# A two-layer gated cross-attention and mixture-of-experts kernel: the last router steps in another order, and identity products between them

## The chip, the core and the metric

The kernel runs on one core of a Trainium2 chip. The metric is the device time of one execution in microseconds (us). The core has five engines that run side by side, each with its own queue of instructions in program order: TensorE (PE, matrix products; its weight loads are shown as PEld), VectorE (DVE), ScalarE (ACT), GpSimd (POOL) and SyncE (SP, which issues most transfers). They wait for each other on semaphores. An instruction that waits holds up everything behind it on its own engine.

## The reference, cut to what matters

The input is `x`, eight sequences of 256 rows with 256 values each, and a context of the same number of rows with 192 values. Two layers follow. Each has a cross-attention with 16 heads and a feed-forward part with eight experts:

```python
x = x + tanh(g_xattn[0]) * L0_xattn(layernorm(x), ctx)
x = x + tanh(g_ffn[0])   * L0_ffn(layernorm(x))       # all 8 experts, 4 weighted, and a shared one
x = x + tanh(g_xattn[1]) * L1_xattn(layernorm(x), ctx)
x = x + tanh(g_ffn[1])   * L1_ffn(layernorm(x))       # 2 of 8 experts for each row
```

The last line is the one that matters here. The router computes eight logits for each row (`layernorm(x) @ Wr + br`), takes the two largest, and weighs them by a softmax. Each row then goes through its two experts, `relu(x @ W1[e] + b1[e]) @ W2[e] + b2[e]`.

## The kernel before

The attention of both layers is cut into 16 units, one for each layer and sequence (`UNITS`), and each unit into eight pairs of heads. For a pair, PE computes the scores by query, DVE takes their row maximum, PE computes the scores by key, ACT takes the exponentials, DVE clips them in the second layer, and PE weighs the values (`weigh_values`, two pairs at a time). Then come `take` (ACT copies the sums), `turn_values` (PE transposes them, DVE divides), `attn_turn` (PE), `project` (PE, then DVE). For the last unit, number 15, the product of `project` is added to `x` on DVE (L1353).

The order of the work is a table, `PLAN`. `make_plan` puts each stage at a half-slot number, and every engine walks through the numbers and issues its own part of each stage. Nothing else decides the order. A slot holds one pair's scores by query, one pair's scores by key, and the stages of two numbers. The scores by key of unit 15 stand in slots 148 to 155.

The second layer's feed-forward part is prepared sequence by sequence. `pick_z` and `stats` finish the row sums and their moments (DVE and POOL), `normal` (ACT) writes the normalized rows, `turn` (PE, copied by ACT) transposes them, `logits1` (PE) multiplies them with the router's weights, and DVE ranks the eight logits and writes `mask` and `picks`. `count1` (PE) adds up on one bank, `by_query[:, 0, :]`, how many rows before each row chose each expert. `weights1` is the softmax, `bias_turn` and `bias1` add the experts' second bias to `x`. `sums` prepares two sums of the last sequence ahead of its projection.

Once all eight sequences are counted, `blocks` and `tables` (DVE) work out which expert each of the 23 blocks of 256 places belongs to, and where each row stands. `stand_at` writes matrices `at_place` that are one where a row stands at a place; `early_places` does that ahead of time for the sequences that are counted by then, `tables` for the rest. A product (L916) turns them into token numbers, POOL gathers the rows, and then the blocks run: `turn_rows`, `up`, `down` (PE), with three products for each matrix product since both sides are split into a high and a low part.

Three banks of PSUM are shared in turn by the small stages (`share_banks`). A stage that takes a bank waits for the stage that had it before.

## Time and profile before

| what | value |
|---|---|
| median of 3 runs | 1027.02 us (1021.71 to 1029.29) |
| the profiled execution | 1020.56 us |
| its span, first to last instruction | 1018.7 us |
| mean granted TensorE clock in it | 0.903 of full |
| PE, DVE, ACT, POOL busy | 89%, 73%, 48%, 24% of the span |

The profile comes from one execution. A row of the timeline gives the start in us from the span's start, the duration in us, the engine, the line of the kernel, the operation, what it writes and reads, and how many instructions are taken together; behind it may stand how long the engine was idle before and what ended the wait. The granted clock is the share of TensorE's full clock of 2.4 GHz: 0.5 is 1.2 GHz. An ordinary float32 product stands in the trace as two instructions, so that x8 means four products.

### The profile page before, as it was taken

What the parts mean: (1) busy time and instruction counts of PE and PEld (TensorE: products, weight loads), DVE (VectorE), ACT (ScalarE), POOL (GpSimd) and SP (SyncE); (2) the same over time, 40 slices, a digit from 0 to 9 for tenths busy, and PEclk for the clock granted to TensorE, in tenths of its full rate; (3) what the DMA queues carried; (4) which work ended last, traced back from release to release, by engine and by line L of the source; (5) the groups of instructions that cost most, each with busy time, mean ns of one, the idle gap of its engine ahead of it and who ended that gap; (6) DMA issues with size and microseconds to landing.
All of it is one profiled execution on the core that took longest, in us unless ns stands there. A gap on an engine that the chain in (4) does not pass through costs nothing.

```text
span 1018.7 us, 18031 instructions
## 1 busy us (share of the span) xinstructions
PE 903.4 (89%) x6385; PEld 735.6 (72%) x6385; DVE 748.5 (73%) x1494; ACT 486.2 (48%) x842; POOL 241.9 (24%) x390
## 2 busy tenths in 40 slices
PE   3578999999999998999888888975699999999995
PEld 2355777777776776677665555643699999999995
DVE  3445667777676768988878789757598888888872
ACT  2135544444534443434434444431376666776762
POOL 5011111020210000101010133320524444444433
PEclk9569899999999999999999766665599999999998
DMA  6967786056154263738374873421666677776642
GB/s 154 167 131 134 173 198 133 25 99 106 43 71 76 45 118 75 140 103 134 85 148 94 220 154 98 122 75 34 235 222 208 212 232 228 231 227 220 208 146 31
DMA packets 129866, 141.52 MB, mean 139 GB/s; under 512 B 12561, under 2 KB 122281, under 8 KB 129649
## 3 DMA queue, kind: packets, MB, share of 16 engines
q1 hardware_dynamic: 119296, 127.59, 51.2%
q0 software_dynamic: 8832, 12.25, 5.6%
q8 instruction: 51, 0.84, 0.4%
q10 hardware_dynamic: 1648, 0.53, 0.2%
q14 instruction: 39, 0.31, 0.1%
HBM read 109.45 MB, written 30.36 MB: 137 GB/s over the span
## 4 chain that ended last, share of the span: by engine, by line
PE 66%; DVE 21%; issue 5%; ACT 3%; POOL 2%; DMA 1%; POOLq 0%; DVEq 0%; ACTq 0%
PE bank L966 12%; PE bank L802 8%; PE by_query L950 7%; PE by_key L950 7%; DVE rowmax L1298 5%; PE bank L812 4%; PE value_bank L744 4%; PE bank L650 4%; PE by_query L707 3%; DVE probs L1323 3%; PE bank L693 3%; PE bank L771 2%; PE bank L659 2%; PE by_key L726 2%; DVE stats L1253 1%
## 5 line engine op out<-in xcount | busy, mean ns | idle before, releaser
L1102 ACT ACTIVATE probs<-by_key 128x1024 f32<-128x1024 f32 x128 | 130.7, 1021 | 92.2 <-PE by_key L726 91.4
L1298 DVE TENSOR_REDUCE rowmax<-by_query 128x4 f32<-128x1024 f32 x128 | 155.4, 1214 | 17.0 <-PE by_query L707 16.9
L1791 POOL TENSOR_SCALAR rstd<-moments 128x2 f32<-128x2 f32 x32 | 10.5, 328 | 514.9 <-DVE moments L1257 514.9
L1851 POOL DMA_INDIRECT out_x<-x,token_i x46 | 78.0, 1695 | 146.8 <-ACT x L1208 139.8
L966 PE MATMUL bank<-w_hi,h_hi 128*128 128x256 f32 x368 | 104.1, 283 | 0.0
L966 PE MATMUL bank<-w_lo,h_hi 128*128 128x256 f32 x368 | 104.1, 283 | 0.0
L966 PE MATMUL bank<-w_hi,h_lo 128*128 128x256 f32 x368 | 104.1, 283 | 0.0
L707 PE MATMUL by_query<-stack_k,stack_q 48*128 48x256 f32 x512 | 70.9, 358 | 35.6 <-DVE rowmax L1298 35.3
L707 PEld LDWEIGHTS by_query<-stack_k,stack_q 48*128 48x128 f32 x512 | 42.8, 206 | 76.7 <-DVE rowmax L1298 46.9
L744 PE MATMUL value_bank<-probs,values 128*32 128x256 f32 x1024 | 79.4, 433 | 8.9 <-DVE probs L1323 8.8
L812 PE MATMUL bank<-w_down,hidden 128*128 128x256 f32 x288 | 79.9, 401 | 3.7 <-DVE summed L1361 1.8
L1323 DVE SCALAR_TENSOR_TENSOR probs<-probs,lower 128x1024 f32<-128x1024 f32 x64 | 77.9, 1218 | 7.1 <-DMA lower<-lower 7.1
L802 PE MATMUL bank<-xnT,w_gate 128*128 128x256 f32 x288 | 78.8, 397 | 3.0 <-DVE lo L1289 2.4
L1135 ACT ACTIVATE act_gate<-bank 128x256 f32<-128x256 f32 x72 | 27.6, 383 | 103.6 <-PE bank L802 103.6
L802 PE MATMUL bank<-xnT,w_up 128*128 128x256 f32 x288 | 74.2, 380 | 0.0
L1456 DVE SCALAR_TENSOR_TENSOR x<-bank,expert_cols,x 128x256 f32<-128x256 f32 x144 | 62.4, 474 | 15.2 <-PE bank L812 15.2
L966 PEld LDWEIGHTS bank<-w_hi,h_hi 128*128 128x128 f32 x368 | 70.7, 192 | 0.0
L966 PEld LDWEIGHTS bank<-w_lo,h_hi 128*128 128x128 f32 x368 | 70.7, 192 | 0.0
L966 PEld LDWEIGHTS bank<-w_hi,h_lo 128*128 128x128 f32 x368 | 70.7, 192 | 0.0
L1720 DVE TENSOR_TENSOR h_lo<-x,h_hi 128x512 fp32r<-128x512 f32 x92 | 63.7, 693 | 3.2
L802 PEld LDWEIGHTS bank<-xnT,w_gate 128*128 128x128 f32 x288 | 52.9, 194 | 15.6 <-DVE lo L1289 3.4
L1690 DVE TENSOR_TENSOR w_lo<-w,w_hi 128x2048 fp32r<-128x2048 f32 x23 | 52.7, 2292 | 15.4 <-ACT w_hi L1173 15.4
(242 smaller groups left out, 2147.7 us busy)
## 6 DMA issues: line engine op xcount, KB each, us to landing
w<-in_L_ffn_W SPq DMA_DIRECT2D x46, 1024.0 KB, 8.7
lower<-lower SPq DMA_DIRECT2D x64, 256.0 KB, 5.3
stack_k<-qk SPq DMA_DIRECT2D x96, 128.0 KB, 5.2
stack_q<-qk SPq DMA_DIRECT2D x96, 128.0 KB, 7.0
qk<-hi SPq DMA_DIRECT2D x31, 256.0 KB, 2.9
qk<-lo SPq DMA_DIRECT2D x31, 256.0 KB, 2.6
rows<-w_gate SPq DMA_DIRECT2D x8, 264.0 KB, 4.6
x<-in_x SPq DMA_DIRECT2D x8, 256.0 KB, 7.0
```

Of the source, the lines that this page charges most:

```text
L707: mm = pe.matmul(by_query[:, side, t * S:t * S + S], sq[rows, p, t * P:t * P + P], sk[rows, p, :], start=True, stop=True)
L744: mm = pe.matmul(value_bank[32 * c:32 * c + 32, o:o + S], values[u % 2][:, kt, 4 * j + c, :], probs[(i + c // 2) % 4][:, kt, c % 2, :], st ...
L802: mm = pe.matmul(bank[:, half * S:half * S + S], w[:, k, e, :], turned_of(("ffn0", b))[:, k, :], start=k == 0, stop=k == 1)
L812: mm = pe.matmul(bank[:, t * D:t * D + D], hidden0[i % 6][:, t * P:t * P + P], w_down0[:, e, :], start=True, stop=True)
L950: mm = pe.matmul(up_bank[pair][:, half * SLOTS:half * SLOTS + SLOTS], wt[:, k, j * P:j * P + P], xt[:, k, :], start=n == 0, stop=n == len( ...
L966: mm = pe.matmul(bank[:, t * D:t * D + D], ht[:, j, t * P:t * P + P], wt[:, j, :], start=j == 0 and t == 0 and n == 0, stop=j == JH - 1 an ...
L1102: ac.activation(probs[i % 4][:, :, :, :].rearrange("p k h s -> p h k s"), by_key[:, :, :].rearrange("p h (k s) -> p h k s", k=2), ACT.Exp) ...
L1298: dv.tensor_reduce(rowmax[u % 2][:, :, p, :], by_query[:, :, :].rearrange("p h (t s) -> p h t s", t=TT), AX, ALU.max).then_inc(sem.max_don ...
L1323: dv.scalar_tensor_tensor(prob, prob, 1.0, bound, ALU.min, ALU.max).then_inc(sem.clip_done, 1)
L1456: op = dv.scalar_tensor_tensor(xt, bank[:, t * D:t * D + D], expert_cols[b % 2][:, t, e:e + 1], xt, ALU.mult, ALU.add)
L1720: dv.tensor_tensor(hl[:, part, :], relu[pair], hh[:, part, :].bitcast(F32), ALU.subtract).then_inc(sem.h_lo, 1)
L1851: po.indirect_dma_start(out[:, :], bass.IndirectOffsetOnAxis(ap=token_i[:, n:n + 1].bitcast(U32), axis=0), ysb[i % 3][:, t, :], None, comp ...
```

## The change

`make_plan` moves the router steps of the last but one sequence, number 6, behind the last unit's values. `EARLY` goes from 14 to 12 row tiles of 128 rows: `early_places` covers six sequences and no longer seven. It is cut in two: part 0 works out the places and writes `at_place` for the first pick, part 1, later, for the second. `bias_turn` and `bias1` of sequence 6 come late, beside those of sequence 7. `sums` comes after the router of sequence 6.

PE gets a new function, `stay_busy`. It issues n products of the identity matrix with itself, 128 rows by 128 columns in float32, into the half `by_query[:, 1, :]` that nobody reads any more. 102 of them are put in: 49 by the table `IDLE_PRODUCTS`, each group ahead of PE's part of the stage that it names, 18 in six groups of three at the ends of slots 150 to 155, and 35 in three groups around the tokens and the first rows. Two banks change places (`turn_bank`, `down_bank`), since the token product now takes another one of the three.

```diff
--- before.py
+++ after.py
@@ -36,7 +36,7 @@
 BLOCKS = NB * S * TOPK1 // SLOTS + E1 - 1
 COLS = BLOCKS * BT
 PICKS = TOPK1 * NT
-EARLY = NT - TT
+EARLY = NT - 2 * TT
 WIDE = D + E1
 CLAMP = 10000.0
 EPS = 1e-5
@@ -63,6 +63,17 @@
 
 FIRST = [("stats", ("query", 0)), ("ctx", 0), ("normal", ("query", 0)), ("gates", 0), ("scale_queries", 0), ("turn", ("query", 0)),
          ("kprod", 0), ("stack_keys", 0), ("qprod", 0), ("stack_queries", 0)]
+
+
+
+IDLE_PRODUCTS = {("turn", ("finish", NB - 2)): 3,
+                 ("logits1", NB - 2): 1,
+                 ("attn_turn", UNITS - 1): 2,
+                 ("project", UNITS - 1): 3,
+                 ("turn", ("finish", NB - 1)): 13,
+                 ("logits1", NB - 1): 2,
+                 ("count1", NB - 1): 9,
+                 ("bias_turn", NB - 1): 16}
 
 
 def layer_of(u):
@@ -141,19 +152,21 @@
         at[g].append(("pick_z", b))
         at[g + 2].append(("stats", ("finish", b)))
         at[g + (9 if b == NB - 1 else 4)].append(("normal", ("finish", b)))
-        at[g + 6 ].append(("turn", ("finish", b)))
-        at[g + 8 ].append(("logits1", b))
-        at[g + 9 ].append(("soft1", b))
-        at[max(g + 10 , 2 * base(UNITS) + 1 + b)].append(("count1", b))
+        behind = 4 if b == NB - 2 else 0
+        at[g + 6 + behind].append(("turn", ("finish", b)))
+        at[g + 8 + behind].append(("logits1", b))
+        at[g + 9 + behind].append(("soft1", b))
+        at[max(g + 10 + 3 * behind // 2, 2 * base(UNITS) + 1 + b)].append(("count1", b))
         if b == NB - 1:
-            at[g - 8].append(("sums", b))
-            at[g - 2].append(("early_places", 0))
+            at[g - 7].append(("early_places", 0))
+            at[g - 2].append(("sums", b))
+            at[g + 5].append(("early_places", 1))
             at[g + 11].append(("blocks", 0))
             at[g + 12].append(("tables", 0))
-        at[g + 11 ].append(("weights1", b))
-        late = 5 if b == NB - 2 else 0
-        at[g + 13 + late].append(("bias_turn", b))
-        at[g + 15 + late].append(("bias1", b))
+        last_but_one = b == NB - 2
+        at[g + (21 if last_but_one else 11)].append(("weights1", b))
+        at[g + (25 if last_but_one else 13)].append(("bias_turn", b))
+        at[g + (31 if last_but_one else 15)].append(("bias1", b))
     return at
 
 
@@ -239,7 +252,7 @@
     value_bank = es.enter_context(nc.psum_tensor("value_bank", [P, 512], F32))
     banks = [es.enter_context(nc.psum_tensor(f"bank{i}", [P, 512], F32)) for i in range(3)]
     up_bank = [by_query[:, 0, :], by_query[:, 1, :], by_key[:, 0, :], by_key[:, 1, :]]
-    turn_bank, down_bank = [value_bank, banks[0]], [banks[1], banks[2]]
+    turn_bank, down_bank = [value_bank, banks[1]], [banks[0], banks[2]]
 
     x = sb("x", [P, NT, D])
     ident = sb("ident", [P, P])
@@ -623,6 +636,11 @@
                 pe.wait_ge(by_name[freed[0]], freed[1])
             return banks[no]
 
+        def stay_busy(n, bank):
+
+            for _ in range(n):
+                pe.matmul(bank[:, 0:P], ident[:, :], ident[:, :], start=True, stop=True)
+
         def ctx(u):
             if layer_of(u):
                 return
@@ -854,7 +872,7 @@
             counts = by_query[:, 0, :]
             if b == 0:
                 pe.wait_ge(sem.max_done, PAIRS * UNITS)
-            if b == NB - 1:
+            if TT * b == EARLY:
                 pe.wait_ge(sem.table_chain, 1)
             pe.wait_ge(sem.mask_ready, b + 1)
             for t in range(TT * b, TT * b + TT):
@@ -900,14 +918,22 @@
                 scores_by_key(u, p)
             for stage, n in PLAN[2 * g]:
                 if stage in stages:
+                    if (stage, n) in IDLE_PRODUCTS:
+                        stay_busy(IDLE_PRODUCTS[stage, n], by_query[:, 1, :])
                     stages[stage](n)
             u, p = divmod(g - base(0) - LAG - 3, PAIRS)
             if 0 <= u < UNITS and p % 2 == 0:
                 weigh_values(u, p // 2)
             for stage, n in PLAN[2 * g + 1]:
                 if stage in stages:
+                    if (stage, n) in IDLE_PRODUCTS:
+                        stay_busy(IDLE_PRODUCTS[stage, n], by_query[:, 1, :])
                     stages[stage](n)
-
+            if base(UNITS - 1) + LAG + 1 < g < base(UNITS) + LAG:
+                pe.wait_ge(sem.max_done, PAIRS * UNITS)
+                stay_busy(3, by_query[:, 1, :])
+
+        stay_busy(10, by_query[:, 1, :])
         pe.wait_ge(sem.tile_no, 2)
         pe.wait_ge(sem.at_place_ready, TOPK1)
         for i, (tile, r) in enumerate((tile, r) for tile in range(NT) for r in range(TOPK1)):
@@ -968,7 +994,9 @@
                                        skip_group_check=True)
             mm.then_inc(sem.down_mm, 1)
 
+        stay_busy(20, by_query[:, 1, :])
         turn_rows(0)
+        stay_busy(5, by_query[:, 1, :])
         up(0, range(0, 2))
         turn_rows(1)
         up(0, range(2, 4))
@@ -1564,16 +1592,19 @@
         def tabled():
             dv.wait_ge(sem.table_chain, chain[0])
 
-        def stand_at(places, first_tile, end):
+        def stand_at(places, first_tile, end, which=range(TOPK1)):
             shape = [P, end - first_tile, P]
-            for r in range(TOPK1):
+            for r in which:
                 dv.tensor_tensor(at_place[:, r, first_tile:end, :], places[:, r, :].unsqueeze(2).broadcast_to(shape),
                                  place_row[:, :].unsqueeze(1).broadcast_to(shape), ALU.is_equal).then_inc(
                     sem.at_place_ready, 1)
 
-        def early_places(_):
-
-            dv.wait_ge(sem.counted, NB - 1)
+        def early_places(part):
+
+            if part:
+                stand_at(early_place[:, :, :], 0, EARLY, range(part, TOPK1))
+                return
+            dv.wait_ge(sem.counted, EARLY // TT)
             dv.wait_ge(sem.qk2_done, PAIRS * UNITS)
             table(dv.tensor_tensor(slots_pick[:, :, 0:EARLY, :], picks[:, :, 0:EARLY, :],
                                    by_query[:, 0, 0:EARLY * E1].rearrange("p (t e) -> p t e", e=E1).unsqueeze(1)
@@ -1588,7 +1619,7 @@
             tabled()
             table(dv.tensor_copy(early_place[:, :, :].rearrange("p r t -> p (r t)"), slot_i[:, 1, 0:TOPK1 * EARLY]))
             tabled()
-            stand_at(early_place[:, :, :], 0, EARLY)
+            stand_at(early_place[:, :, :], 0, EARLY, range(1))
 
         def blocks(_):
             dv.wait_ge(sem.counted, NB)
```

How PE's queue looks from the scores of unit 15's last pair but one on. Before (`bank<-wr,xnT` are the logits of `logits1`, `bank<-ident,w_gate 128x128` is the turn of the normalized rows of sequence 6, `bank<-ident,weighted` the turn of the values, `bank<-ident,attn` is `attn_turn`, and `bank<-wo,attnT` the projection):

```order
L726 MATMUL by_key<-stack_q,stack_k 128x256 x4
L744 MATMUL value_bank<-probs,values 32x256 x8
L684 MATMUL bank<-ident,w_gate 128x128 x4
L849 MATMUL bank<-wr,xnT 128x8 x4
L744 MATMUL value_bank<-probs,values 32x256 x8
L861 MATMUL by_query<-mask,tri 128x8
...
L754 MATMUL bank<-ident,weighted 128x128 x4
L763 MATMUL bank<-ident,attn 128x128 x4
L771 MATMUL bank<-wo,attnT 128x256 x4
```

Now, with the identity products as `by_query<-ident`:

```order
L744 MATMUL by_key<-stack_q,stack_k 128x256 x4
L762 MATMUL value_bank<-probs,values 32x256 x8
L642 MATMUL by_query<-ident 128x128 x3
L762 MATMUL value_bank<-probs,values 32x256 x8
L642 MATMUL by_query<-ident 128x128 x3
L702 MATMUL bank<-ident,w_gate 128x128 x4
L772 MATMUL bank<-ident,weighted 128x128 x4
L642 MATMUL by_query<-ident 128x128
L867 MATMUL bank<-wr,xnT 128x8 x4
L642 MATMUL by_query<-ident 128x128 x2
L781 MATMUL bank<-ident,attn 128x128 x4
L642 MATMUL by_query<-ident 128x128 x3
L789 MATMUL bank<-wo,attnT 128x256 x4
```

The last values went ahead of the turn and the logits of sequence 6, the turn of the values ahead of the logits, and the count of sequence 6 (`mask,tri`) behind the projection.

PE's queue from the turn of the last sequence (`bank<-ident,w_up`) to the tokens. Before:

```order
L684 MATMUL bank<-ident,w_up 128x128 x4
L849 MATMUL bank<-wr,xnT 128x8 x4
L861 MATMUL by_query<-mask,tri 128x8
...
L876 MATMUL bank<-ident,w_gate 8x128 x2
L884 MATMUL bank<-b,wT 128x256 x2
L916 MATMUL bank<-in_tile_no,at_place 128x92 x32
```

Now:

```order
L642 MATMUL by_query<-ident 128x128 x13
L702 MATMUL bank<-ident,w_up 128x128 x4
L642 MATMUL by_query<-ident 128x128 x2
L867 MATMUL bank<-wr,xnT 128x8 x4
L894 MATMUL bank<-ident,w_gate 8x128 x2
L642 MATMUL by_query<-ident 128x128 x9
L879 MATMUL by_query<-mask,tri 128x8
...
L642 MATMUL by_query<-ident 128x128 x16
L894 MATMUL bank<-ident,w_gate 8x128 x2
L902 MATMUL bank<-b,wT 128x256 x4
L642 MATMUL by_query<-ident 128x128 x10
L942 MATMUL bank<-in_tile_no,at_place 128x92 x32
```

Fifty identity products came in here (13, 2, 9, 16 and 10), and two sequences' bias products (x4) stand ahead of the tokens instead of one's.

DVE's queue behind unit 15's last clip, up to the row sums of the last sequence. Before, the router and the early places (both picks) ran there, the places behind the divided values (`attn<-bank,recip`) and right ahead of the projection's sum (L1353):

```order
L1323 SCALAR_TENSOR_TENSOR probs<-probs,lower 128x1024 x2
L1528 TENSOR_TENSOR route_0<-bank,br 128x16
...
L1335 TENSOR_TENSOR attn<-bank,recip 128x2x128
...
L1570 TENSOR_TENSOR at_place<-early_place,place_row 128x1792 x2
L1353 SCALAR_TENSOR_TENSOR x<-bank,tg,x 128x512
```

Now:

```order
L1351 SCALAR_TENSOR_TENSOR probs<-probs,lower 128x1024 x2
L1609 TENSOR_TENSOR slots_pick<-picks,by_query 128x2x96
...
L1598 TENSOR_TENSOR at_place<-early_place,place_row 128x1536
...
L1363 TENSOR_TENSOR attn<-bank,recip 128x2x128
L1556 TENSOR_TENSOR route_0<-bank,br 128x16
...
L1381 SCALAR_TENSOR_TENSOR x<-bank,tg,x 128x512
...
L1598 TENSOR_TENSOR at_place<-early_place,place_row 128x1536
L1553 SCALAR_TENSOR_TENSOR route_1<-bank,rstd,br 128x8 x2
```

One of the two early place matrices now stands ahead of the divided values and the other behind the projection's sum.

## Rows read from the trace of the kernel before

**Rows 1.** The page: busy time by engine, and granted clock in 40 slices

```profile
PE 903.4 (89%) x6385; PEld 735.6 (72%) x6385; DVE 748.5 (73%) x1494; ACT 486.2 (48%) x842; POOL 241.9 (24%) x390
PEclk9569899999999999999999766665599999999998
```

**Rows 2.** Windows, PE: stretch, length, busy (instructions), granted clock, DMA share, GB/s

```profile
646.80:670.50 23.70, 23.20 (x141) 0.50 0.53 130
670.70:677.40 6.70, 5.28 (x43) 1.00 0.39 110
677.50:697.90 20.40, 13.41 (x68) 0.50 0.11 32
701.40:735.40 34.00, 18.59 (x102) 0.50 0.47 158
```

**Rows 3.** Timeline, unit 15's last clips to its projection, all engines

```profile
678.60 2.35 DVE L1323 SCALAR_TENSOR_TENSOR probs<-probs,lower 128x1024 f32<-128x1024 f32 x2
681.94 1.09 ACT L1062 ACTIVATE w_gate<-x,rstd 128x256 f32<-128x256 f32 x2 [4.24 <-POOL rstd L1798]
683.17 1.08 PE L684 MATMUL bank<-ident,w_gate 128*128 128x128 f32 x4 [3.10 <-ACT w_gate L1062]
685.10 1.85 PE L849 MATMUL bank<-wr,xnT 128*128 128x8 f32 x8 [0.84 <-ACT xnT L1079]
686.87 1.94 PE L744 MATMUL value_bank<-probs,values 128*32 128x256 f32 x16
688.94 0.60 ACT L1109 ACTIVATE weighted<-value_bank 128x512 f32<-128x512 f32 x1 [3.99 <-PE value_bank L744]
689.68 1.09 PE L754 MATMUL bank<-ident,weighted 128*128 128x128 f32 x4 [0.29 <-ACT weighted L1109]
...
693.66 3.75 PE L771 MATMUL bank<-wo,attnT 128*128 128x256 f32 x8 [0.84 <-ACT attnT L1116]
693.74 3.96 DVE L1570 TENSOR_TENSOR at_place<-early_place,place_row 128x1792 bf16<-128x1792 f32 x2
697.62 0.74 DVE L1353 SCALAR_TENSOR_TENSOR x<-bank,tg,x 128x512 f32<-128x512 f32 x1
```

**Rows 4.** Timeline, PE at the full clock, shortly before

```profile
672.33 1.07 PE L744 MATMUL value_bank<-probs,values 128*32 128x256 f32 x16
674.82 0.66 PE L754 MATMUL bank<-ident,weighted 128*128 128x128 f32 x4
```

**Rows 5.** Timeline, from the last sequence's turn to its count

```profile
701.13 0.92 PE L684 MATMUL bank<-ident,w_up 128*128 128x128 f32 x4 [1.59 <-DVE w_up L1262]
702.89 1.85 PE L849 MATMUL bank<-wr,xnT 128*128 128x8 f32 x8 [0.84 <-ACT xnT L1079]
704.95 0.36 DVE L1525 SCALAR_TENSOR_TENSOR route<-bank,rstd,br 128x8 f32<-128x8 f32 x2 [3.36 <-PE bank L849]
707.20 0.17 PE L861 MATMUL by_query<-mask,tri 128*128 128x8 bf16 x1 [2.46 <-DVE mask L1537]
```

**Rows 6.** Timeline, from the last bias turn to the first rows

```profile
711.20 0.59 PE L876 MATMUL bank<-ident,w_gate 128*8 128x128 f32 x2 [3.73 <-DVE w_gate L1551]
712.40 2.04 PE L884 MATMUL bank<-b,wT 8*128 8x256 f32 x4 [0.61 <-ACT wT L1042]
716.28 0.75 DVE L1570 TENSOR_TENSOR at_place<-place_tile,place_row 128x256 bf16<-128x256 f32 x2
716.42 2.63 PE L916 MATMUL bank<-in_tile_no,at_place 128*128 128x92 bf16 x32 [1.98 <-DVE in_tile_no L1639]
717.22 0.68 DVE L1510 TENSOR_TENSOR x<-bank,x 128x512 f32<-128x512 f32 x1
718.99 3.60 PE L923 MATMUL bank<-onehotT,b 8*128 8x23 f32 x16
719.10 0.39 DVE L1679 TENSOR_SCALAR tok<-bank,spare_row 128x23 f32<-128x23 f32 x2 [1.20 <-PE bank L916]
726.97 1.12 PE L934 MATMUL value_bank<-ident,xs_in 128*128 128x128 f32 x4 [4.37 <-DMA xs_in<-rows,token_i]
```

**Rows 7.** Chain of waits: two equal groups of the first block's products

```profile
729.50 5.49 PE by_query L950 x24
...
735.72 2.87 PE by_key L950 x24
```

## The prediction

> **What bounds the kernel now.** I read the page first [rows 1]: PE is busy for 89% of the span, and its granted clock is full or nearly so except in the first slices and in a stretch from slice 24 to 29. The change acts in that stretch alone. The windows [rows 2] cut it up: the clock is 0.50 from 646.8 to 670.5 us although PE is busy for 23.20 of 23.70 us, 1.00 for the next 6.7 us, and 0.50 again from 677.5 to 697.9 and from 701.4 to 735.4 us. So a first stretch is bound by PE at half its clock, and two others are chains through several engines in which PE works and waits by turns, also at half clock.
>
> The timeline gives the chain [rows 3]. DVE ends the last clip at 680.95 (678.60 + 2.35). The last values could start then. But PE stands at the turn of sequence 6, which needs ACT's normalized rows (681.94 + 1.09), and the values wait behind turn and logits until 686.87. From the last clip to the projection's sum on DVE (697.62) it takes 16.67 us. Then the last sequence's sums, turn, logits and router follow [rows 5], the tables, the tokens, the gather and the first products [rows 6].
>
> **What an identity product costs.** No such product is in the trace before. The nearest row is the projection, also float32 on the full array: four products of 256 columns take 3.75 us at half clock [rows 3], 0.94 each. Half the columns make 0.47 us, and 0.23 at full clock. The lower bound is a transpose of 128 columns: 1.09 / 4 = 0.27 us at half clock [rows 3] and 0.66 / 4 = 0.17 at full clock [rows 4]. I take 0.47 and 0.23, since a transpose is another kind of instruction. 102 products are then 24 us of PE at full clock and 48 at half. Most of it lies in waits; what it does to the time depends on the clock that is granted, so I work out each term at both.
>
> **A, slots 150 and 151.** Two groups of three stand ahead of unit 14's projection, and PE is the bound there [rows 2]. At half clock they add 6 x 0.47 = 2.8 us. If they bring the clock up one step earlier, some 6 us of PE at half clock are halved, less the groups themselves at mixed clock: about -1.4. The other four groups stand where PE waits anyhow (5.28 busy of 6.70 us [rows 2]), in 1.4 us of gaps, and I count them at nothing if the clock is full. I take 0, between the ends.
>
> **B, from the last clip to the projection's sum.** Counted from the last clip's end, at full clock: values until 1.2 (1.07 us [rows 4]); three products; the turn of sequence 6, which needs ACT's rows at 2.1 (683.03 - 680.95), until 2.9; the turn of the values (0.66) until 3.5; DVE is then busy with the early places until about 3.2 (small steps of 1.5 us together, and one matrix of 1536 columns for 3.96 / 2 x 1536 / 1792 = 1.7 us), so nothing waits for it; one product, the logits (half of 1.85) until 4.7; two products; `attn_turn` until 5.8; ACT's copy (0.60 and 0.1 for the hand-over) until 6.5, with three products beside it; the projection (half of 3.75) until 8.4. The sum starts at 8.6 instead of 16.67: -8.1 us. The router of sequence 6 and the two sums need about 3.5 us of DVE from 4.8 on, and end before 8.6. At half clock the same walk gives 2.1, 3.5, 4.6, 5.7, 8.0 (one product and the logits), 10.1 (two products, `attn_turn`), 11.5 (three products outlast ACT) and 15.3: -1.4 us. A half-clock piece inside a mostly full stretch costs 1 to 2 us. I take -7.0, nearer the full clock, since the gaps that PE has now (7.0 of 20.4 us idle [rows 2]) are nearly all filled or closed.
>
> **C, the last turn and logits.** Now 7.33 us from the sum to the ranks [rows 5]. At full clock the turn saves 0.3 and the logits 0.9: -1.2. Thirteen products (3.0 us) fit behind the count of sequence 6 into the 3.5 us between 697.62 and 701.13. The second early matrix ends about 5.9 us after the sum and the logits reach DVE at 6.1, so it is hidden, barely; it is late next. At half clock thirteen products take 6.1 us and the turn starts 2.8 late. I take -0.6.
>
> **D, the count.** PE waits 2.46 us for the mask [rows 5]. Nine products and the bias turn of sequence 6 take 2.4 at full clock and 4.8 at half: 0 to +2.4. I take +0.4.
>
> **E, the tokens.** They start at 716.42, when DVE's `in_tile_no` is done [rows 6]. Ahead of them PE now has, from 707.4 on, sixteen products (3.7), the bias turn (which needs 711.2 anyhow), two bias products instead of one, ACT's copy between them, and ten products. At full clock that ends about 717, hidden but for 0.4 us, and then the tokens take 1.4 instead of 2.63. DVE meanwhile has two matrices of 512 columns (0.65 each instead of 0.37) and two additions of 0.68 [rows 6], and reaches `tok` at 719.25 instead of 719.10: +0.15. But the clock is 0.50 all through this stretch in the trace, the bias products in it included (2.04 us for two) [rows 2, 6], and the change puts more of them there. With the clock down there, the ten products take 4.7 us, the tokens start at 719 to 720 and take up to 2.6: +1.9 to +3.3. At half clock in all of it, with sixteen products of 7.5 us, the tokens start 8.6 us late. I take +1.9.
>
> **F, the first rows.** From the tokens' end (719.05) to the rows' arrival (726.97) there are 7.9 us that PE does not set [rows 6]. The bias products of the first layer of experts (3.60 at half clock, 1.8 at full) and twenty products (4.6 or 9.4) stand there: 6.4 us fit, 13.0 are 5.1 too many. Behind it the turn saves 0.5 at full clock and the first 24 products take 2.87 instead of 5.49 [rows 7]: -3.1 together. With the clock down at first and up later, the fill ends 2 to 3 us late and takes nearly all of that back. I take -1.7. From 735.5 on the clock is full in both and nothing changes.
>
> **Sum.** 0 - 7.0 - 0.6 + 0.4 + 1.9 - 1.7 = -7.0 us. The profiled execution took 1020.56 us, which makes 1013.6. It is 6.5 us below the median of the three runs shown, so against that median the forecast is 1027.0 - 7.0 = **1020 us**. SP's queue has the same transfers, two of them later and off the chain; POOL's is unchanged.
>
> **The rule on the clock, weighed.** In this trace the clock stood at 0.50 for 23.7 us of nearly unbroken PE work and rose only behind it [rows 2]. The Trainium skill (TensorE: Matmul & The Clock Gate, section "Why this matters for your kernels") says that an idle gap between bursts of products is what puts the clock down, and that back-to-back work keeps it up. The trace does not bear that out, since the busy stretch was at half clock too. By the rule the filled stretch would be at full clock throughout, which is the second case below.
>
> **Rivals.**
> 1. *Mixed clock*, the sum above: -3 to -11 us, 1016 to 1024. For it: every fill is sized for the full clock, but the rows at 0.50 include stretches in which PE had little idle time. Chance 0.50.
> 2. *Full clock nearly everywhere.* A -1.4, B -8.1, C -1.2, D 0, E +0.15, F -3.1: -13.6 us, 1013. This is what the rule named above would do. For it: a late fill at half clock makes its own stretch dense, and dense stretches are where the clock rose [rows 2, 7]. Against it: 646.8 to 670.5 was dense too. Chance 0.27.
> 3. *The fill gives back what the order gains.* The last values start 5.8 us earlier (686.87 to 681.05), but with the clock down in most of A and B, nine products stand on B's path. A +2.0, B -3.0, C 0, D +0.4, E +1.9, F 0: +1.3, that is 0 to +3 us, 1027 to 1030. For it: half clock is what three of four windows show [rows 2]. Chance 0.16.
> 4. *Slower.* Identity products do not raise the clock at all, like the transposes and values around 683 to 693 us [rows 2, 3], and every group longer than its wait delays what stands behind it on PE. A +2.8, B -1.4, C +2.8, D +2.4, E +8.6, F +5.1 and 0.9 for the five products behind the turn: +21 us, 1048. It decides as soon as thirteen products take over 3.1 us and sixteen with ten over what DVE's tables leave. Against it: those transposes stood between gaps, and the clock rose in the first block's unbroken products, 5.49 us for 24 of them and then 2.87 [rows 7]. Chance 0.07.
>
> **How the numbers follow.** The forecast is case 1's. Cases 1 and 2 and most of 3 must be in the range: 1010 to 1030 us, which leaves out case 4 and the tails. A difference under 1% (10.3 us) cannot be told from no change in this kernel. Faster by over 1% is below 1016.8: most of case 2 and a little of case 1, 0.29. Slower by over 1% is case 4, 0.07. The rest is 0.64.
>
> **What would show it.** In the new profile the last values should start within 0.3 us of the last clip, and the projection's sum 8 to 10 us behind that clip rather than 16.7 (B). An identity product should show as two instructions of together 0.23 or 0.47 us. Granted clock 1.00 between the last clip and the count says B and C are right; 0.50 in the bias products of sequences 6 and 7 and late tokens say E is; PE still in its twenty products when the rows land says that F is nearer 0. A clock of 0.50 throughout the fill would mean case 4. The forecast is wrong if the stretch ahead of unit 14's projection moves by more than the 2.8 us of A, or if the new places on DVE, not PE, set the ranks of the last sequence.

## The result

The changed kernel takes **1019.36 us** (median of 14 runs, 1009.17 to 1033.51) against 1026.41 us (14 runs, 1021.33 to 1030.36). The ratio is 0.9906, 95% interval [0.9877, 0.9936]. A second set (experiment 9) gave 1018.66 us (12 runs) against 1027.11 and 0.9879 [0.9844, 0.9914]. The medians count all runs; the ratios, here and below, leave out slow ones, those more than 1.5% above the fastest run of their kernel. The forecast against the median was 1020 us, a change of -7.0; measured were -7.1 and -8.5.

The profiled execution took 1020.99 us, no less than that of before (1020.56). Yet it holds the gain, and to see that one has to know where to measure. The page first, against [rows 1]:

```profile
PE 923.8 (91%) x6589; PEld 756.7 (74%) x6589; DVE 750.2 (74%) x1494; ACT 486.0 (48%) x842; POOL 241.4 (24%) x390
PEclk9667899999999999999999856769899999999998
```

PE is busy 20.4 us longer, in 204 more instructions. The granted clock is now low in slices 24 to 27 instead of 24 to 29. Then the windows of PE that answer to [rows 2] (stretch, length, busy time with instructions, granted clock, DMA share, GB/s):

```profile
675.00:682.30 7.30, 7.30 (x48) 0.67 0.51 151
682.30:691.40 9.10, 8.20 (x78) 1.00 0.33 82
691.40:700.00 8.60, 7.99 (x69) 1.00 0.00 1
700.00:709.60 9.60, 7.70 (x71) 1.00 0.09 30
...
716.20:719.90 3.70, 3.70 (x21) 0.65 0.84 290
...
723.50:729.90 6.40, 6.40 (x42) 0.73 0.21 60
```

From the sum of unit 14's projection on, the clock is full except in the ten products ahead of the tokens and the start of the tokens, and again in part of the twenty products; the experts' bias products between them run at full clock (1.96 us for 16 instructions, 3.60 before [rows 6]). I measure from unit 15's first scores by key to the first product of `down`. Before, this takes 93.11 us (651.51 to 744.62), now 84.71 (660.66 to 745.37): 8.4 us less. But the stretch began 9.15 us later, in a part that the change does not touch, where the clock stood lower in this execution (0.90 on average ahead of the stretch, 0.91 before). Behind `down` both need 274 us. The pieces, against the profile of before (a projection's sum is DVE's addition of it, the ranks are DVE's first step on the logits (`route`), the count is DVE's reading of it):

| piece | before | after | change | predicted |
|---|---|---|---|---|
| A, first scores to the sum of unit 14's projection | 20.39 | 21.69 | +1.3 | 0 |
| that sum to the last clip's end | 9.06 | 9.05 | 0 | 0 |
| B, last clip to the sum of unit 15's projection | 16.66 | 8.65 | -8.0 | -7.0 |
| C, sum to ranks | 7.33 | 7.10 | -0.2 | -0.6 |
| D, ranks to count | 2.57 | 2.48 | -0.1 | +0.4 |
| E, count to `tok` | 11.58 | 12.18 | +0.6 | +1.9 |
| `tok` to the first rows' turn | 7.87 | 9.02 | +1.15 | 0 |
| F, that turn to the second 24 products | 8.51 | 5.40 | -3.1 | -1.7 |

**B** in the timeline of the changed kernel, the rows that answer to [rows 3]:

```profile
689.04 2.35 DVE L1351 SCALAR_TENSOR_TENSOR probs<-probs,lower 128x1024 f32<-128x1024 f32 x2
691.45 1.07 PE L762 MATMUL value_bank<-probs,values 128*32 128x256 f32 x16 [0.93 <-DVE probs L1351]
692.41 1.09 ACT L1090 ACTIVATE w_gate<-x,rstd 128x256 f32<-128x256 f32 x2 [2.72 <-POOL rstd L1829]
692.45 0.94 PE L642 MATMUL by_query<-ident 128*128 128x128 f32 x6
693.64 0.63 PE L702 MATMUL bank<-ident,w_gate 128*128 128x128 f32 x4 [0.26 <-ACT w_gate L1090]
695.11 1.03 PE L867 MATMUL bank<-wr,xnT 128*128 128x8 f32 x8
697.96 1.96 PE L789 MATMUL bank<-wo,attnT 128*128 128x256 f32 x8 [0.17 <-ACT attnT L1144]
700.04 0.75 DVE L1381 SCALAR_TENSOR_TENSOR x<-bank,tg,x 128x512 f32<-128x512 f32 x1 [0.37 <-PE bank L789]
```

The last values start 0.06 us behind the last clip (691.39) instead of 5.9 us. The three identity products (x6, since each is two instructions) take 0.94 us while ACT's rows are still on their way. The turn, the logits and the projection take little over half of what they took [rows 3], and before the projection PE waits 0.17 us instead of 0.84. **C**, against [rows 5]:

```profile
699.92 3.15 PE L642 MATMUL by_query<-ident 128*128 128x128 f32 x26
704.11 1.75 DVE L1598 TENSOR_TENSOR at_place<-early_place,place_row 128x1536 bf16<-128x1536 f32 x1
704.40 1.52 POOL L1825 TENSOR_TENSOR rstd<-rstd 128x2 f32<-128x2 f32 x1
705.04 1.03 PE L867 MATMUL bank<-wr,xnT 128*128 128x8 f32 x8 [0.39 <-ACT xnT L1107]
707.15 0.36 DVE L1553 SCALAR_TENSOR_TENSOR route<-bank,rstd,br 128x8 f32<-128x8 f32 x2 [1.29 <-POOL rstd L1829]
```

The logits are there at 706.07, 6.0 us behind the sum as worked out. The ranks wait 1.1 us more, for POOL: its step of 128x2 at 704.40 takes 1.52 us, beside DVE's new matrix. The first **gather**, then, against [rows 6]:

```profile
719.91 1.86 PE L942 MATMUL bank<-in_tile_no,at_place 128*128 128x92 bf16 x32
721.80 0.39 DVE L1710 TENSOR_SCALAR tok<-bank,spare_row 128x23 f32<-128x23 f32 x2 [0.66 <-PE bank L942]
723.05 2.29 DVE L1721 TENSOR_TENSOR w_lo<-w,w_hi 128x2048 fp32r<-128x2048 f32 x1 [0.26 <-issue]
723.69 0.32 ACT L1242 ACTIVATE b_all<-bank 128x184 f32<-128x184 f32 x1 [1.07 <-PE bank L949]
723.74 2.71 POOL L1869 DMA_INDIRECT xs_in<-rows,token_i  x1 [16.73 <-DVE token_i L1717]
725.85 2.29 DVE L1721 TENSOR_TENSOR w_lo<-w,w_hi 128x2048 fp32r<-128x2048 f32 x1 [0.50 <-ACT w_hi L1201]
726.75 2.24 POOL L1869 DMA_INDIRECT xs_in<-rows,token_i  x1 [0.30 <-issue]
730.83 0.66 PE L960 MATMUL value_bank<-ident,xs_in 128*128 128x128 f32 x4 [0.88 <-DMA xs_in<-rows,token_i]
```

Both issues that the first rows need now stand beside one of DVE's subtractions and take 2.71 and 2.24 us; before, they took 2.86 and 0.98. PE waits 0.88 us for the rows although it had its twenty products. In the chain of waits the answer to [rows 7]:

```profile
732.89 3.14 PE by_query L976 x24
...
736.47 2.87 PE by_key L976 x24
```

### The profile page after: what moved, and what is told of

Same layout as the page of the kernel before. It is cut to its first block, busy times and chain, and to the rows that moved or that the text cites. A ratio compares the mean times of both kernels' runs of the same rounds, so it can differ in the third digit from the quotient of the medians.

```text
span 1019.3 us, 18439 instructions
## 1 busy us (share of the span) xinstructions
PE 923.8 (91%) x6589; PEld 756.7 (74%) x6589; DVE 750.2 (74%) x1494; ACT 486.0 (48%) x842; POOL 241.4 (24%) x390
## 4 chain that ended last, share of the span: by engine, by line
PE 67%; DVE 19%; issue 5%; ACT 3%; POOL 3%; DMA 2%; SPq 0%; POOLq 0%; DVEq 0%; ACTq 0%
PE bank L992 12%; PE bank L820 9%; PE by_query L976 7%; PE by_key L976 6%; DVE rowmax L1326 5%; PE value_bank L762 5%; PE bank L830 4%; PE bank L668 4%; PE by_query L725 4%; DVE probs L1351 3%; PE bank L711 3%; PE bank L677 2%; PE bank L789 2%; PE by_key L744 2%; DVE stats L1281 1%
## 5 line engine op out<-in xcount | busy, mean ns | idle before, releaser
L1130 ACT ACTIVATE probs<-by_key 128x1024 f32<-128x1024 f32 x128 | 130.6, 1020 | 98.4 <-PE by_key L744 97.9
L1822 POOL TENSOR_SCALAR rstd<-moments 128x2 f32<-128x2 f32 x32 | 10.5, 327 | 517.4 <-DVE moments L1285 517.4
L830 PEld LDWEIGHTS bank<-w_down,hidden 128*128 128x128 f32 x288 | 50.7, 193 | 17.0 <-issue 3.7
```

The costliest lines, as they stand in the source:

```text
L830: mm = pe.matmul(bank[:, t * D:t * D + D], hidden0[i % 6][:, t * P:t * P + P], w_down0[:, e, :], start=True, stop=True)
L1130: ac.activation(probs[i % 4][:, :, :, :].rearrange("p k h s -> p h k s"), by_key[:, :, :].rearrange("p h (k s) -> p h k s", k=2), ACT.Exp) ...
```

## The experiments

**1. The order alone.** `stay_busy` is empty, all else is as in the changed kernel.

```diff
-            for _ in range(n):
+            for _ in range(0):
                 pe.matmul(bank[:, 0:P], ident[:, :], ident[:, :], start=True, stop=True)
```

> The new order and the early places in two parts, without one identity product. If order and clock both carry the change, the stretch from the last clip's end to the projection's sum shrinks from 16.7 us to about 12 us (values 2.1, turn 3.2, turn of the values 4.3, logits 6.2, attention turn 7.3, copy 8.0, projection 11.7, all at half clock) and not to the 8.7 us of the changed kernel; the first rows keep their 8.5 us up to the second half of the first products; the time is 4 to 5 us below before, ratio about 0.996. If the order alone carries it, the stretch is near 8.7 us and the ratio near 0.991.

Measured: ratio 0.9923 [0.9887, 0.9958] (10 runs). In its profile B takes 9.93 us, between the two values expected, and the first rows are as before (E 11.60, F 8.39). C takes 7.15 us, as in the changed kernel. The profiled execution took 1033.22 us, with a low clock in the unchanged part ahead; B is read from mark to mark. PE's timeline in B:

```profile
704.84 1.03 PE L867 MATMUL bank<-wr,xnT 128*128 128x8 f32 x8 [0.20 <-ACT xnT L1107]
...
707.20 3.28 PE L789 MATMUL bank<-wo,attnT 128*128 128x256 f32 x8 [0.84 <-ACT attnT L1144]
```

So 6.7 of B's 8.0 us are the order's, by this one profile. About 5 of them are the new order at half clock, as the walk worked out ahead of the run has it (11.7 us); the rest is clock. The logits run at the full clock (1.03) without any filling, and the projection falls back to half clock within its first microsecond (granted 0.98 from 704.4 to 707.8 us, 0.50 from there to 710.6).

**2. The filling alone.** The table, the groups and `stay_busy` are put into the kernel before.

```diff
+                    if (stage, n) in IDLE_PRODUCTS:
+                        stay_busy(IDLE_PRODUCTS[stage, n], by_query[:, 1, :])
...
+        stay_busy(20, by_query[:, 1, :])
         turn_rows(0)
+        stay_busy(5, by_query[:, 1, :])
         up(0, range(0, 2))
```

> The identity products in the old order. If order and clock both carry the change, the clock is up behind the last clip, but the projection's sum stays about 15 us behind it, since the values wait behind the turn and both early place matrices stand ahead of the sum on DVE; the first rows gain their 3.1 us as in the changed kernel; ratio 0.995 to 0.997. If the products carry it all, the stretch is near 9 us and the ratio near 0.991. If products only cost, the ratio is over 1.000.

Measured: 0.9882 [0.9822, 0.9942] (4 runs), lower than the 0.995 to 0.997 expected. B is 15.09 us, as expected, since the values still stand behind the turn and the logits:

```profile
687.39 0.63 PE L699 MATMUL bank<-ident,w_gate 128*128 128x128 f32 x4 [2.42 <-ACT w_gate L1087]
...
689.81 1.66 PE L759 MATMUL value_bank<-probs,values 128*32 128x256 f32 x16
```

The gain is elsewhere: A 16.93 us, C 6.24 (no early matrix there, all of C at the full clock, POOL's steps behind the first three 0.19 to 0.20), E 10.44, F 5.33; the way from `tok` to the rows' turn takes 9.68, 1.8 more. The whole stretch takes 84.45 us, as much less as the changed kernel's in its first profile, but 3.5 us of that are A, which differs between executions of one kernel too (experiment 5).

Without A, the order alone makes the stretch 7.1 us shorter, the filling alone 5.2, and both together 9.6. In B the two add up (6.7 and 1.6, together 8.0). They get in each other's way in C and E: the filling alone shortens these by 1.1 each, but the new order puts DVE's matrix into C, and into E a second sequence's bias products, behind which the ten products delay the tokens (they start 10.28 us behind the count in the changed kernel, 8.92 with the filling alone). By the times alone the three kernels cannot be told apart, since their intervals overlap.

**3. Transposes in place of products**, the same number.

```diff
-                pe.matmul(bank[:, 0:P], ident[:, :], ident[:, :], start=True, stop=True)
+                pe.transpose(bank[:, 0:P], ident[:, :], ident[:, :])
```

> The changed kernel with a transpose of the identity in place of each identity product, at the same 102 places. If any work of the full array keeps the clock up, the granted clock from the last clip to the count is 1.00 as in the changed kernel and the time is the same within 1 us or a little less, since a transpose is shorter. If transposes do not count for the clock (the Trainium skill says so of them, TensorE: Matmul & The Clock Gate, Part 4), the clock is 0.5 there, the stretch from the last clip to the sum is 12 to 13 us instead of 8.7, and the rows gain nothing: 5 to 7 us slower than the changed kernel.

Measured: 0.9898 [0.9853, 0.9943] (4 runs). The clock is 1.00 through B, which takes 8.06 us. It falls in C: thirteen transposes last 1.62 us where thirteen products last 3.15, and the longer gap behind them is followed by a turn and logits near half clock.

```profile
692.71 1.62 PE L642 MATMUL by_query<-ident 128*128 128x128 f32 x13
696.37 0.98 PE L702 MATMUL bank<-ident,w_up 128*128 128x128 f32 x4 [2.04 <-DVE w_up L1290]
...
698.19 1.85 PE L867 MATMUL bank<-wr,xnT 128*128 128x8 f32 x8 [0.41 <-ACT xnT L1107]
```

F takes 8.58 us, as long as before, so the first rows gain nothing here: twenty transposes are through 2.1 us before the rows land.

**4. More groups, from slot 147 on.** `LAG - 2` stands for `LAG + 1` in the condition of the slots, nine products more.

> The changed kernel with groups of three identity products from slot 147 on instead of slot 150, nine more products. If the half clock of the stretch ahead of unit 14's projection is what bounds it, the clock rises there and the stretch from unit 15's first scores by key to that projection shrinks from 21.7 us to 16 to 19 us: 3 to 5 us faster than the changed kernel. If the clock does not rise earlier, nine products of 0.47 us add 4 us in that stretch, and the time is 4 us above the changed kernel.

Measured: 0.9894 [0.9811, 0.9976] (4 runs), not to be told from the changed kernel; A 18.70 us, B, C and D as in the changed kernel. The 18.70 lies in the first theory's range, but with the same groups A takes 20.44 us in experiment 11, so they do not bring it.

**5. No groups in the slots** (18 products fewer).

```diff
-            if base(UNITS - 1) + LAG + 1 < g < base(UNITS) + LAG:
-                pe.wait_ge(sem.max_done, PAIRS * UNITS)
-                stay_busy(3, by_query[:, 1, :])
```

> The changed kernel without the 18 products at the ends of slots 150 to 155. If they cost as predicted, the stretch from unit 15's first scores by key to the projection of unit 14 is near the 20.4 us of before where the clock stays at half, and 1.3 us shorter than in the changed kernel at the same clock. If they are what keeps the clock up behind the last clip, the clock there falls to 0.5 to 0.8 and the stretch from the last clip to the sum grows from 8.7 to 9.5 to 12 us. If they do neither, both stretches are as in the changed kernel.

Measured: 0.996 [0.9928, 0.9992] (8 runs); A 19.79, B 10.35 us. E takes 13.78 us, and a delay behind the rows adds 5.2 us to the stretch (see experiment 7), so not all of the higher time is the groups'. PE's windows:

```profile
644.30:661.20 16.90, 16.57 (x105) 0.50 0.43 102
661.20:664.40 3.20, 3.20 (x29) 0.99 0.89 252
664.40:674.00 9.60, 8.30 (x42) 0.51 0.50 131
...
683.10:688.50 5.40, 5.36 (x32) 0.50 0.00 0
```

The clock rises at 661.2, 7 us behind unit 15's first scores, by itself, and is lost again 3.2 us later. It is at half again in the first 5.4 us of B, although the products of `IDLE_PRODUCTS` stand there and PE is busy for 5.36 of them: the full clock in B rests on the slots' groups ahead of it as well. In the second profile of the changed kernel (experiment 9) it rises at the same place, 7 us behind unit 15's first scores (658.97), and stays up:

```profile
649.00:665.80 16.80, 16.27 (x105) 0.51 0.41 103
666.00:676.00 10.00, 9.40 (x81) 0.99 0.63 143
676.00:685.00 9.00, 8.15 (x77) 1.00 0.61 139
```

In its first profile it rises only 19 us behind them (660.66), which is where it also rises in the kernel before, without any filling (670.7 against 651.51 [rows 2]):

```profile
655.70:680.00 24.30, 23.92 (x152) 0.51 0.44 125
680.00:709.60 29.60, 26.18 (x226) 1.00 0.19 51
```

The groups do not always keep it. In experiment 11, with nine products more, it rises 7.6 us behind the first scores (658.49) and falls once more for 3.3 us:

```profile
672.90:676.20 3.30, 3.30 (x25) 0.50 0.79 89
```

**6. No products around the tokens and the rows** (the groups of 10, 20 and 5 left out).

> The changed kernel without the last 35 products (ten ahead of the tokens, twenty and five around the first rows). If they buy the full clock for the first rows, the stretch from the rows' turn to the second half of the first products grows from 5.4 to about 8.5 us. If the bias products alone decide the clock at the tokens, the tokens start earlier, 8.9 us behind the count instead of 10.3, and take 2.6 us. Net 1 to 3 us slower than the changed kernel. If they only cost, it is 1 us faster.

Measured: 0.9943 [0.9897, 0.9988] (8 runs). The count to `tok` takes 11.59 us, as before, so the ten products cost 0.6. F takes 8.52 us, so the 35 products are worth 3.1 there; and `tok` to the rows' turn takes 7.93 instead of 9.02. Together they save 1.4 us in the stretch. The ratio's interval overlaps that of the changed kernel's first set (up to 0.9936).

**7. The early matrix of the second pick later**, with the last tables.

```diff
-            at[g + 5].append(("early_places", 1))
...
+            stand_at(early_place[:, :, :], 0, EARLY, range(1, TOPK1))
             stand_at(place_tile[:, 0, :]
```

> The changed kernel with the early matrix of the second pick moved from behind the last projection's sum to the tables, right ahead of the late matrices. If that matrix is what made one of GpSimd's steps of the last sequence take 1.52 us instead of 0.20, the stretch from the sum to the ranks falls from 7.1 to 6.2 us and the step to 0.2 us; the tokens are read 1 to 1.7 us later behind the count in exchange. If GpSimd's step was slow for another reason, the stretch stays at 7.1 us.

Measured: 0.9966 [0.9925, 1.0007] (8 runs). C is 6.23 us: without DVE's matrix POOL's step is short, and the ranks wait for PE's logits alone.

```profile
699.08 0.19 POOL L1825 TENSOR_TENSOR rstd<-rstd 128x2 f32<-128x2 f32 x1
...
700.89 0.36 DVE L1552 SCALAR_TENSOR_TENSOR route<-bank,rstd,br 128x8 f32<-128x8 f32 x2 [2.09 <-PE bank L866]
```

The 0.9 us are lost again in E (13.11 us against 12.18), where the matrix now stands. Behind the rows this kernel and that of experiment 5 need 14.3 to 14.4 us from the second 24 products to `down`; the kernels before and changed need 9.1 to 9.3. ACT's first two bias steps in that stretch come late:

```profile
731.35 0.84 ACT L1225 ACTIVATE x<-by_query,b_all 128x256 f32<-128x256 f32 x2 [4.26 <-PE by_query L975]
735.56 0.84 ACT L1225 ACTIVATE x<-by_query,b_all 128x256 f32<-128x256 f32 x2 [3.37 <-PE by_key L975]
```

They start 3.5 and 7.7 us behind the first of those products; in the changed kernel 1.8 and 3.2 us. What holds ACT there is open: the profile shows no instruction that it waits for. It puts 5.2 us into the profiles of these two kernels that do not belong to what was taken out of them.

**8. The first gather without DVE beside it.** The second subtraction goes behind `split_rows(0)`, and the first waits until POOL has issued the first block's gathers. The `memset` writes the same constant once more and serves as the signal.

```diff
-        for i in range(4):
+        gather(0)
+        po.memset(minus_half[:, :], -0.5).then_inc(sem.ident_ready, 1)
+        for i in range(1, 4):
             gather(i)
...
+        dv.wait_ge(sem.ident_ready, CONSTANTS + 1)
         split_w1(0)
-        split_w1(1)
         split_rows(0)
+        split_w1(1)
```

> The changed kernel, but VectorE starts its first low part of the experts' weights only once GpSimd has issued the first block's two gathers, and the second low part comes behind the split of the first rows. In the changed kernel the two gathers took 2.71 and 2.24 us to issue, each beside such a low part, against 0.95 to 1.24 us alone. If VectorE's low part is what slows GpSimd's issue, the two take about 1.2 and 1.0 us and the stretch from the tokens' reading to the first rows' turn falls from 9.0 to 6.3 to 6.8 us: 2 us or more faster than the changed kernel, if the twenty products do not then end later than the rows. If the slow issue has another cause (the transfers or the products on TensorE), it stays at 2.2 to 2.7 us and the stretch at 8 to 9 us.

Measured: 0.9828 [0.9737, 0.9918] in four runs, median 1011.95 us.

```profile
713.81 1.24 POOL L1870 DMA_INDIRECT xs_in<-rows,token_i  x1 [16.73 <-DVE token_i L1717]
715.35 0.97 POOL L1870 DMA_INDIRECT xs_in<-rows,token_i  x1 [0.30 <-issue]
...
720.41 2.28 DVE L1721 TENSOR_TENSOR w_lo<-w,w_hi 128x2048 fp32r<-128x2048 f32 x1
721.34 2.18 POOL L1870 DMA_INDIRECT xs_in<-rows,token_i  x1 [0.30 <-issue]
724.79 0.66 PE L960 MATMUL bank<-ident,xs_in 128*128 128x128 f32 x4 [1.41 <-DMA xs_in<-rows,token_i]
```

The issues take 1.24 and 0.97 us, and the rows come 6.35 us behind `tok` instead of 9.02. But the second block's rows are late in turn (PE waits 1.41 us), and from the count to `down` it is 35.99 us against 35.74. The gain of 2.7 us is given back up to `down`: F takes 6.98 us instead of 5.40, and from the second 24 products to `down` it is 10.48 instead of 9.14. This kernel's lower time had to come from elsewhere: in its profile A is 16.80 us, the case of experiment 9.

**9 to 11. The changed kernel, experiment 8's and a union of 4 and 8, on one chip.**

> The changed kernel itself, unchanged, so that the two kernels beside it can be compared with it on one chip. Theory 1 (the gain is the stretch between the last clip and the sum, about 8 us): ratio 0.990 to 0.993 to the kernel before. Theory 2 (part of the 0.983 of the kernel with the first gather alone is that the full clock comes earlier before unit 14's projection, which differs from execution to execution): the median here falls within 3 us of that kernel's repeat, and executions at a mean granted clock of 0.925 to 0.93 are the ones near 1012 us.

> The kernel in which the first gather has DVE to itself, once more. In its profile the rows came 6.35 us behind the first of the token tables instead of 9.02, but the second block's rows and the second weight subtraction came later, and the way from the count to the second products was 36.0 us against 35.7. Theory 1 (gain given back): no difference to the changed kernel on the same chip, within 2 us. Theory 2 (the gain stands, as the medians 1012 and 1019 suggest): 3 to 8 us below it.

> The first gather alone on DVE and POOL, and groups of three identity products from slot 147 on instead of 150. If more products early bring the full clock earlier, as one profile suggested (18.70 us to unit 14's projection instead of 21.69): 2 to 4 us below the changed kernel, 1013 to 1017. If the time to the projection is set by where in the unchanged first part the clock stands, which the products do not reach: as the changed kernel plus their own 0 to 1 us, 1017 to 1022.

| kernel | ratio to before | runs | whole stretch | A |
|---|---|---|---|---|
| changed | 0.9879 [0.9844, 0.9914] | 12 | 80.23 us | 17.03 |
| first gather alone | 0.9899 [0.9862, 0.9937] | 6 | 80.31 us | 16.91 |
| union of both | 0.9898 [0.985, 0.9947] | 6 | 82.42 us | 20.44 |

None differs from the changed kernel beyond the intervals. The medians are 1018.66, 1014.58 and 1018.47 us: the first gather alone lies 4.1 us lower, as the second theory of experiment 10 had it, but its ratio to the kernel before is no lower, so the gain is not shown. The 0.9828 of experiment 8 rests on four runs, three of them between 1011 and 1012.6 us, and did not come again. Experiment 11 came out as its second theory had it: more groups did not shorten A. In the changed kernel's 26 runs the nine below 1016 us have a mean granted clock of 0.923 to 0.933, and the nine above 1021.3 us one of 0.912 to 0.922. No other version was shown to be faster.

**12. The kernel before, once more.**

> The kernel before, profiled once more, for what its clock does from unit 15's scores to the first down products (93.1 us in the first profile). If the low clock there comes from its own waits, the granted clock from the last clip to the projection's sum is again 0.50 to 0.6 and that interval 15 to 16.7 us, wherever the full clock ends in the part before. If it differs as much as the interval from unit 15's first scores to unit 14's projection does between executions of the changed kernel (16.8 to 21.7 us), it can come out anywhere from 9.9 to 16.7 us, and the gain read from one pair of profiles is partly chance.

The stretch takes 93.27 us (93.11 in the first profile), B 16.66 again, with the clock at 0.50 again:

```profile
685.60:702.30 16.70, 11.40 (x52) 0.50 0.05 18
```

So the slow clock in B belongs to the kernel before, not to one execution. A is 20.45 us, against 20.39.

## Why the prediction was right, point by point

The time is right (-7.1 and -8.5 us, forecast -7.0), and B, which carried it, is right in mechanism. That the medians agree to 0.1 and 1.5 us is luck. Without A the pieces of the profile come to -9.7 us where the forecast's terms, A being 0, come to -7.0; A moves the stretch by another +1.3 or -3.4; and the part ahead of the stretch, which the change leaves as it is, begins it anywhere from 651.5 to 660.7 us in the profiles of the two kernels.

- **A, forecast 0 between -1.4 and +2.8: the mechanism was incomplete.** The first profile shows +1.3: the groups run at half clock, as costed. The second shows -3.4, outside the bounds and more than the 2.8 us that the prediction named as a sign of being wrong. The same code has two patterns here: in one the full clock ends 5 us ahead of unit 15's first scores and comes back 19 us behind them, in the other it ends 10 us ahead and comes back 7 us behind. Four more profiles of kernels with the same code up to there (experiments 6, 7, 8 and 10) give A as 18.66, 21.70, 16.80 and 16.91 us. The groups bring the clock back in neither pattern: the first of them stands 9 to 10.5 us behind the scores, and the later rise is there before too. That they keep it up after an early rise is likely but not shown: A took 19.79 us without them (experiment 5) and 16.8 to 17.0 with them, but 20.44 with still more of them (experiment 11). What decides between the patterns shows itself ahead of the scores, in the unchanged part, and stays open.
- **B, forecast -7.0: measured -8.0, the full-clock walk (-8.1) within 0.1 us.** In nine profiles of the new order with all of the slots' groups, B is 8.06 us (with transposes) or 8.64 to 8.65. The 1 us that I had put on a piece at half clock did not come. The working for half clock had only the order together with the nine products, -1.4; the order alone brings 6.7 (experiment 1), about 5 of them at half clock already. The products add 1.3, and for that they need the slots' groups ahead of them: without those B is 10.35 (experiment 5), longer than with no filling at all.
- **C, forecast -0.6: -0.2, the wrong thing was late next.** PE and the second matrix ended as worked out. I had named DVE's matrix as late next and left out POOL's chain of small steps, which it lengthens (1.52 instead of 0.20 us). So not PE but a new place on DVE, through POOL, sets the ranks, the other sign of being wrong that the prediction named. Experiment 7 shows the -1.1 without it.
- **D, forecast +0.4: -0.1.** Nine products at full clock are hidden.
- **E, forecast +1.9: +0.6, a term sized too high.** The low clock that I feared stands only in the ten products (0.65) and the start of the tokens, and these take 1.86 instead of 2.63 us [rows 6]. Left out altogether (experiment 6), the ten products change E by 0.6.
- **The gather, counted at nothing, costs 1.15 us.** I had taken the 7.9 us from the tokens' end to the rows as work "that PE does not set". PE does set part of it: bias products at full clock free ACT, ACT then has the second half's high part sooner, DVE's second subtraction starts 2.8 us after the first instead of 4.3, and it falls on POOL's second issue. With those products at half clock (experiments 1 and 6) that issue takes 0.97 us. That DVE's subtraction is what lengthens it is shown by experiment 8; the chain from PE over ACT is read from the rows.
- **F, forecast -1.7: -3.1, the full-clock value.** The twenty products were through when the rows landed.

**The cases.** The first (mixed clock) had -3 to -11 us and holds both medians; by the clock the truth lies between it and the second (-13.6): full from the clip to the bias turn, mixed around it. The third and fourth needed the half clock under the filling and did not occur. **The rule that was weighed** (the Trainium skill, TensorE: Matmul & The Clock Gate, section "Why this matters for your kernels") does better than I gave it from the last clip on, where the filled stretch is at full clock. Busy work alone did not raise the clock, though: 16.57 of 16.90 us were busy at 0.50 (experiment 5), and in experiment 11 it fell for 3.3 us in which PE was never idle, after 6.7 us of which 6.1 were busy.

## What to carry to other kernels

A stretch in which an engine waits and works by turns at half clock can be won in two ways, by closing the waits or by filling them. Add the two gains piece by piece, not as totals: here they added up in B, but in C and E the new order put work where the filling had gained. Compare such kernels from mark to mark within the stretch that the change touches, over several profiles: the whole times of the changed kernel's executions differ by 24 us, the change is 7 to 8. And when an engine becomes faster, list whose instructions are moved onto a neighbour's: here two of DVE's landed on POOL's.

## What the runs showed of the hardware

- **DVE beside POOL.** A subtraction of 128x2048 (2.29 us) lengthens POOL's indirect issue from 0.95 to 1.24 us to between 2.0 and 2.9 us, and a matrix of 128x1536 a POOL step of 128x2 from 0.20 to 1.52 us, until 0.06 us behind the matrix's end. The Trainium skill (SBUF — State Buffer, section "SBUF: two separate sides") says that the two share a pair of ports, that a DVE instruction with two inputs in SBUF takes it against a POOL instruction that reads SBUF, and that whichever starts first holds it for its whole instruction. Both DVE operations here have two inputs in SBUF, and these rows agree.
- **Transposes among products held a full clock**: 1.00 through B in experiment 3, with every filling product and the turns as transposes. No run shows it rising on transposes alone. The Trainium skill (TensorE: Matmul & The Clock Gate, section "Part 4: PE-mode transpose") says that the full clock does not engage for them; in this mixture of transposes and products it does.
- An identity product of 128 columns in float32 takes 0.24 us at the full clock (3.15 / 13) and 0.50 at half (1.49 / 3, the first group of the slots in the first profile), close to the 0.23 and 0.47 estimated from the projection; a transpose takes 0.12 at the full clock (1.62 / 13).
